# A layer's attention in another order: one block of scores per tile, signals per pair of heads, the adding of x on GpSimd

## The reference

```python
def _L3_xattn_ref(q, k, v, gamma):
    h = N_HEAD                              # 8
    qh = q.reshape(B, h, dq, Lq); kh = k.reshape(B, h, dq, Lk); vh = v.reshape(B, h, dv, Lk)
    qk = jnp.einsum('bhdq,bhdl->bhql', qh, kh) * scale
    sm = jax.nn.softmax(qk, axis=-1)
    ret = jnp.einsum('bhql,bhdl->bhdq', sm, vh)
    return gamma * ret.reshape(B, Dv, Lq)

x = x + jnp.tanh(g_xattn[3]) * _L3_xattn_ref(_layernorm(x, axis=-1), ctx_2048, ctx_2048, L3_xattn_gamma)
```

## Time and profile before

| what | value |
|---|---|
| median of 3 runs | 2855.9 us (2855.89 to 2860.24) |
| the profiled execution, its own time | 2857.04 us |
| its span | 2855.2 us |
| TensorE busy over the span | 2451.8 us (86%) |
| VectorE, ScalarE, GpSimd busy | 2037.1, 1296.4, 1179.1 us |
| mean granted clock of TensorE | 0.931 |
| first score matmul of the stage | at 2593.03 us |
| last statistics of the stage | start at 2818.46 us |

### The profile page before, as it was taken

The page is one execution under the profiler, slowest core; times in us unless marked ns, Lnnn a source line. Parts: engine busy times, 40 slices in busy tenths (PEclk is TensorE's granted clock), DMA queues, the critical chain, the costliest instruction groups (busy, mean ns, idle before and its releaser), DMA issues. The chain is left out here.

```text
span 2855.2 us, 51398 instructions
## 1 busy us (share of the span) xinstructions
PE 2451.8 (86%) x17090; PEld 2057.1 (72%) x17090; DVE 2037.1 (71%) x5105; ACT 1296.4 (45%) x3941; POOL 1179.1 (41%) x2615
## 2 busy tenths in 40 slices
PE   5758999939999999999999869999699997466997
PEld 2346777728888888888888858888588886234775
DVE  7964555558888888888888847777554554895776
ACT  0013333236666666666666623333144443344663
POOL 4401000037777777777777711111143443122112
PEclk9768999969999999999999969999799999676998
DMA  2030000010000000000000030000100000001000
GB/s 73 17 133 24 16 16 8 1 63 3 3 3 5 3 3 3 3 3 3 3 5 1 1 106 23 23 23 12 52 7 9 7 5 1 0 1 53 21 24 31
DMA packets 29155, 56.72 MB, mean 20 GB/s; under 512 B 4846, under 2 KB 22574, under 8 KB 27422
## 3 DMA queue, kind: packets, MB, share of 16 engines
q1 hardware_dynamic: 28894, 53.43, 5.7%
HBM read 51.33 MB, written 2.10 MB: 19 GB/s over the span
## 5 line engine op out<-in xcount | busy, mean ns | idle before, releaser
L434 PE MATMUL bank<-m_xr,m_wgr 128*88 128x512 f32 (+1 forms) x1824 | 442.3, 395 | 17.4 <-POOL m_wgr L494 17.4
L434 PEld LDWEIGHTS bank<-m_xr,m_wgr 128*88 128x88 f32 (+1 forms) x1824 | 307.3, 172 | 116.9 <-issue 19.5
L742 PE MATMUL bank<-l_w,l_xq 128*128 128x128 f32 (+1 forms) x2048 | 358.5, 328 | 9.9 <-DVE l_xq L906 7.1
L742 PEld LDWEIGHTS bank<-l_w,l_xq 128*128 128x128 f32 x2048 | 300.4, 192 | 31.1 <-DVE l_xq L906 7.5
L985 DVE TENSOR_SCALAR xn_T<-xn_T,l_tiny 128x128 f32<-128x128 f32 x768 | 297.2, 453 | 8.4 <-POOL l_tiny L1026 8.4
L494 POOL TENSOR_TENSOR m_wgr<-m_wg,m_wgr 128x512 fp32r<-128x512 f32 (+1 forms) x28 | 40.3, 1440 | 585.5 <-ACT m_wgr L472 585.5
L855 ACT ACTIVATE l_qt<-bank,l_head_b,l_head_w 128x256 f32<-128x256 f32 x256 | 144.6, 565 | 287.5 <-PE bank L787 287.5
L447 PEld LDWEIGHTS bank<-m_wdr,m_hbr 88*128 88x128 f32 (+1 forms) x1824 | 233.1, 192 | 26.9 <-DVE m_hbr L549 18.0
L447 PE MATMUL bank<-m_wdr,m_hbr 88*128 88x256 f32 (+1 forms) x1824 | 239.5, 285 | 10.1 <-DVE m_hbr L549 10.0
L582 DVE SCALAR_TENSOR_TENSOR x_resident<-bank,m_cg,x_resident 128x256 f32<-128x256 f32 x448 | 185.9, 478 | 85.4 <-PE bank L447 79.4
L484 ACT ACTIVATE m_sg<-bank 88x512 f32<-88x512 f32 (+1 forms) x152 | 90.8, 597 | 323.0 <-PE bank L434 323.0
(11 more groups left out here) (272 smaller groups left out, 5715.2 us busy)
## 6 DMA issues: line engine op xcount, KB each, us to landing
l_w<-in_l_w SPq DMA_DIRECT2D x1, 6144.0 KB, 17.3
m_wg<-in_m_gu SPq DMA_DIRECT2D x18, 256.0 KB, 2.6
m_wg<-in_m_gu SPq DMA_DIRECT2D x10, 352.0 KB, 2.9
l2f_w<-in_l_w SPq DMA_DIRECT2D x3, 1024.0 KB, 7.5
m_wd<-in_m_down SPq DMA_DIRECT2D x18, 128.0 KB
x_resident<-in_x SPq DMA_DIRECT2D x4, 512.0 KB, 5.6
l_ctxT<-in_ctxT SPq DMA_DIRECT2D x1, 2048.0 KB, 7.1
l_toep<-in_l_toep SPq DMA_DIRECT2D x16, 128.0 KB, 2.0
```

The source lines that it names most:

```text
L434: r = e.matmul(banks[2 * (q % 2) + half][0:M, :], WGR[:, u % 2, a, k, sub, half, :], XR[:, b, k, cols], start=k == 0 and n == 0, stop=k == ...
L742: e.matmul(bank[:, to:to + width], XQ[:, v, k, :], W[:, k, g, at:at + width], start=k == 0, stop=k == KT - 1)
```

## The change

What it does:

- TensorE issues the scores of all four pairs of a tile in one block of 16 instructions, with `o` as the outer loop. It waits for all exponentials of the tile before.
- Maxima and exponentials are signalled for each pair, four times a tile instead of twice; the first two transpose blocks need the first two pairs only.
- TensorE's order of a step is: two transpose blocks, the next tile's scores, half the values of the tile before, two transpose blocks, the other half. Its pipeline has two tiles in it instead of three.
- VectorE copies block 0 instead of block 3; ScalarE copies 1, 2 and 3, block 3 between the exponentials of the next tile. VectorE's order is four maxima, that copy, the division, then a normalisation or statistics.
- Each tile has its own bank for values, in turn, in place of each batch.
- x is added on GpSimd, behind its cutting of queries and masking of values; the statistics come later.

```diff
-            s_score = signals("scored", 2 * N)
-            s_max = signals("maximum", 2 * N)
-            s_exp = signals("exponent", 2 * N)
+            s_score = signals("scored", N)
+            s_max = signals("maximum", PAIRS * N)
+            s_exp = signals("exponent", PAIRS * N)
...
                 begin(e, ends)
                 for b in range(B):
                     if b >= 2:
-                        e.wait_ge(*s_score(4 * (b - 1)))
+                        e.wait_ge(*s_score(2 * (b - 1)))
                     e.dma_start(CK[:, b % 2, :], A["ctx"][b]).then_inc(s_ck.of(b), 16)
                     if b >= 2:
                         e.wait_ge(*s_cv(b - 1))
                     e.dma_start(CT[:, b % 2, :, :], A["ctxT_b"][b]).then_inc(s_ct.of(b), 16)
...
-            def score(e, n, half):
...
                 if n >= 1:
-                    e.wait_ge(*s_exp(2 * n - 1 + half))
+                    e.wait_ge(*s_exp(PAIRS * n))
                 for o in range(2):
-                    for p in (2 * half, 2 * half + 1):
+                    for p in range(PAIRS):
...
             def turn(e, n, j):
-                e.wait_ge(*s_exp(2 * n + 2))
-                if j >= 2:
-                    e.wait_ge(*s_pte(3 * n + j - 1))
-                elif n >= 1:
-                    e.wait_ge(*(s_pte(3 * n) if j == 0 else s_pte_v(n)))
+                e.wait_ge(*s_exp(PAIRS * n + 2 * a + 2))
+                if j == 0 and n >= 1:
+                    e.wait_ge(*s_pte(3 * (n - 1) + 2))
+                if j == 1 and n >= 1:
+                    e.wait_ge(*s_pte(3 * n))
+                if j == 2:
+                    e.wait_ge(*s_pte_v(n + 1))
+                if j == 3:
+                    e.wait_ge(*s_pte(3 * n + 1))
...
-            def values(e, n):
...
-                e.wait_ge(*s_pte(3 * n + 3))
-                e.wait_ge(*s_pte_v(n + 1))
-                e.wait_ge(*s_cv(b + 1))
-                if qt == 0 and b >= 2:
-                    e.wait_ge(*s_mix(2 * (b - 1)))
-                for o in range(2):
-                    for k in range(KT):
-                        for at, weights in ((0, CV), (D, colm)):
-                            for p in range(PAIRS):
...
+            def values(e, n, o):
+
+                b = n // 2
+                if o == 0:
+                    e.wait_ge(*s_pte(3 * n + 3))
+                    e.wait_ge(*s_pte_v(n + 1))
+                    e.wait_ge(*s_cv(b + 1))
+                    if n >= 2:
+                        e.wait_ge(*s_mix(n - 1))
+                for k in range(KT):
+                    for at, weights in ((0, CV), (P, colm)):
+                        for p in range(PAIRS):
+                            rows = slice(32 * p, 32 * p + 32)
+                            w = CV[:, b % 2, o, k, rows] if weights is CV else colm[:, o, rows]
+                            r = e.matmul(pacc[n % 2][rows, at:at + P], w, PT[:, n % 2, k, 2 * p + o, :],
+                                         start=o == 0 and k == 0 and weights is CV, stop=o == 1 and k == 1 and weights is colm)
+                if o == 1:
+                    r.then_inc(s_pv.sem, 1)
...
             def tensor(e):
                 begin(e, ends)
-                score(e, 0, 0)
-                for s in range(N + 2):
+                score(e, 0)
+                for s in range(N + 1):
                     if s < N:
-                        score(e, s, 1)
-                    if 1 <= s <= N:
-                        turn(e, s - 1, 0)
-                        turn(e, s - 1, 1)
-                    if s >= 2:
-                        values(e, s - 2)
-                    if 1 <= s <= N:
-                        turn(e, s - 1, 2)
+                        turn(e, s, 0)
+                        turn(e, s, 1)
                     if s + 1 < N:
-                        score(e, s + 1, 0)
-                    if 1 <= s <= N:
-                        turn(e, s - 1, 3)
-
-            def exponent(e, n, half):
-                e.wait_ge(*s_max(2 * n + half + 1))
+                        score(e, s + 1)
+                    if s >= 1:
+                        values(e, s - 1, 0)
+                    if s < N:
+                        turn(e, s, 2)
+                        turn(e, s, 3)
+                    if s >= 1:
+                        values(e, s - 1, 1)
+
+            def exponent(e, n, p):
+                e.wait_ge(*s_max(PAIRS * n + p + 1))
                 if n >= 2:
-                for h in range(4 * half, 4 * half + 4):
...
+                for h in (2 * p, 2 * p + 1):
...
                 r.then_inc(s_exp.sem, 1)
...
-                if j < 3:
+                if j == 0:
+                    e.tensor_copy(to, turned[j % 2][:, :]).then_inc(s_pte_v.sem, 1)
+                else:
                     e.copy(to, turned[j % 2][:, :]).then_inc(s_pte.sem, 1)
-                else:
-                    e.tensor_copy(to, turned[j % 2][:, :]).then_inc(s_pte_v.sem, 1)
 
             def scalar(e):
                 begin(e, ends)
                 for s in range(N + 1):
                     if s < N:
                         exponent(e, s, 0)
-                    if s >= 1:
-                        keep_turned(e, s - 1, 0)
-                    if s < N:
                         exponent(e, s, 1)
                     if s >= 1:
-                        keep_turned(e, s - 1, 1)
-                        keep_turned(e, s - 1, 2)
-
-            def maximum(e, n, half):
-                e.wait_ge(*s_score(2 * n + half + 1))
+                        keep_turned(e, s - 1, 3)
+                    if s < N:
+                        exponent(e, s, 2)
+                        exponent(e, s, 3)
+                        keep_turned(e, s, 1)
+                        keep_turned(e, s, 2)
+
+            def maximum(e, n, p):
+                e.wait_ge(*s_score(n + 1))
                 if n >= 2:
-                    e.wait_ge(*s_exp(2 * (n - 2) + half + 1))
-                for p in (2 * half, 2 * half + 1):
-                    r = e.tensor_reduce(negmax[:, n % 2, 2 * p:2 * p + 2], scores[p][:, :].rearrange("p (o k) -> p o k", o=2),
-                                        AXX, ALU.max, negate=True)
-                r.then_inc(s_max.sem, 1)
-
-            def finish(e, n):
-                b, qt = n // 2, n % 2
-                cols = slice(qt * P, (qt + 1) * P)
+                    e.wait_ge(*s_exp(PAIRS * (n - 2) + p + 1))
+                e.tensor_reduce(negmax[:, n % 2, 2 * p:2 * p + 2], scores[p][:, :].rearrange("p (o k) -> p o k", o=2),
+                                AXX, ALU.max, negate=True).then_inc(s_max.sem, 1)
+
+            def divide(e, n):
                 e.wait_ge(*s_pv(n + 1))
-                e.reciprocal(rinv[:, n % 2, :], pacc[b % 2][:, D + qt * P:D + (qt + 1) * P]).then_inc(s_inv.sem, 1)
+                e.reciprocal(rinv[:, n % 2, :], pacc[n % 2][:, P:2 * P]).then_inc(s_inv.sem, 1)
                 e.wait_ge(*s_inv(n + 1))
                 if n >= 2:
                     e.wait_ge(*s_xadd(n - 1))
-                e.scalar_tensor_tensor(mixed[:, n % 2, :], pacc[b % 2][:, cols], gam[:, 0:1], rinv[:, n % 2, :],
+                e.scalar_tensor_tensor(mixed[:, n % 2, :], pacc[n % 2][:, 0:P], gam[:, 0:1], rinv[:, n % 2, :],
                                        ALU.mult, ALU.mult).then_inc(s_mix.sem, 1)
-                e.wait_ge(*s_mix(n + 1))
-                e.tensor_tensor(X[:, b, cols], X[:, b, cols], mixed[:, n % 2, :], ALU.add).then_inc(s_xadd.sem, 1)
-                if qt == 1:
-                    e.wait_ge(*s_xadd(n + 1))
-                    e.bn_stats(stats[:, b, :], X[:, b, :]).then_inc(bn.sem, 1)
...
-                for s in range(N + 2):
-                    if s == 0:
-                        maximum(e, 0, 0)
+                for s in range(N + 4):
                     if s < N:
-                        maximum(e, s, 1)
-                    if s >= 2:
-                        finish(e, s - 2)
+                        for p in range(PAIRS):
+                            maximum(e, s, p)
+                        keep_turned(e, s, 0)
+                    if 2 <= s < N + 2:
+                        divide(e, s - 2)
                     if s % 2 == 1 and s // 2 + 2 < B:
                         normalise(e, s // 2 + 2)
-                    if s + 1 < N:
-                        maximum(e, s + 1, 0)
-                    if 1 <= s <= N:
-                        keep_turned(e, s - 1, 3)
+                    if s >= 4 and s % 2 == 0:
+                        b = s // 2 - 2
+                        e.wait_ge(*s_xadd(2 * b + 2))
+                        e.bn_stats(stats[:, b, :], X[:, b, :]).then_inc(bn.sem, 1)
...
             def gpsimd(e):
                 begin(e, ends)
-                for b in range(B):
...
+                separate(e, 0)
+                for s in range(N + 2):
+                    if s % 2 == 0 and s // 2 + 1 < B:
+                        separate(e, s // 2 + 1)
+                    if s >= 2:
```

(47 more changed lines are left out.)

1 line of the change is left out of this document (removed).

## The result

The changed kernel takes **2864.76 us**, the kernel before in the same runs 2857.82 (14 runs each): a ratio of 1.0025, 95% interval 1.0016 to 1.0033, or 6.9 us slower. The forecast was 3.8 slower, 2859.7, with a range of 2851 to 2873 that holds the result. Of its three cases the result falls, with 6.9, just beyond the line of 5.7 us: into "slower", which had 0.42, and not into "within", which had 0.48. Of the 5.1 us between 2859.7 and 2864.76 the change makes up 3.1; the other 1.9 are the kernel before, whose median is 2857.82 in these 14 runs and was 2855.9 in the three that the forecast started from.

The account below looks back on a forecast made before the run. TensorE bound the stage before; afterwards a TensorE–ScalarE ring of 6.85 us a step would. Steps +7.1, start -0.5, end -2.8 give +3.8 us on the 2855.9 median: 2859.7, range 2851 to 2873.

Parts of the forecast that it names:

- the line of 5.7 us: About 0.2% of the kernel's time, what a measurement of this kernel can tell from no change; passed with steps over 6.92.
- slower: Whole kernel: slower than before by more than 5.7 us; chance 0.42.
- within: Whole kernel: within 5.7 us of the time before; chance 0.48.
- The ring: Fourth layer's attention: TensorE and ScalarE wait for each other through ScalarE's second copy; 6.85 us a step instead of 6.595.
- TensorE's own work: Per step after the change: scores 1.10, values 2.00, transposes 2.12, together 5.22 us; not the bound.
- The rivals with poor overlap: Score blocks: four groups run in full succession, 2889 us, chance 0.03, or overlap in part, 2867 us, chance 0.06.
- the rival: TensorE's idle 1.6 us a step lowers the clock; about 2902 us, or 2865 to 2875 for a few steps; chance 0.10.
- Start and end: Stage's first and last tiles, partly at 1.2 GHz: start -0.5 us, end -2.8 us, as the pipeline is a step shorter.
- VectorE fits: VectorE's maxima, copy, division and normalisation or statistics fit inside the step, covered by 1.4 us of slack.
- GpSimd's add: Adding x on GpSimd, between 0.29 and 0.73 us, is hidden in each step; only the last tile's lies on the path.
- The rival on the faster side: TensorE stays the bound with steps of 5.2 to 5.6 us: 2815 up to 2826 us; chance 0.08.

## Why the prediction was right, and where it was off

**The ring.** It was named link by link, in the right order, and every link is in the timeline. 6.85 was forecast, 6.93 measured. The 0.08 come mostly from one choice: for the last four exponentials I took the row at 2711.46, 1.57 long, while those that follow a copy directly are the row at 2707.13, 1.61; measured 1.62. The rest is a hundredth here and there, in the scores, the values, the transposes and the first copy. 28 x 0.08 = 2.3 us.

**TensorE's own work and the four row groups.** The block of 16 scores takes 1.15 us from its first start to its last end, where a half block of 8 took 1.13. To what follows it is 1.11, forecast 1.10. The rivals with poor overlap, 2867 and 2889, are out. The Trainium skill (TensorE: Matmul & The Clock Gate, Part 3, Measured speedup vs the span model) gives a speedup of 3.07 for four row tiles. That isn't what these rows show: 8 instructions on two groups took 1.07 to what follows, so 16 on one group would take 4 x 1.07 = 4.28 if two groups overlap fully, and 4.28 / 3.07 = 1.39, as an estimate from the page's figure, is 0.28 longer than the 1.11 measured.

**The clock.** This is the step that failed, in part: the sum has nothing for a fall of the clock, and two cost 3.1 us. The forecast had 1.00 in the middle of the stage and gave the rival 0.10, with "a few such steps give 2865 to 2875". It came in its mild form, in two of the 28 steps from tile 3 to tile 31, with 1.57 each. My argument against it was that TensorE had been far idler where the clock had fallen before, 1.19 busy of 3.40 us, than 5.2 of 6.85. That is an average over a step, and within a step the idle time is bunched: just ahead of the fall at 2685.40 it was busy 1.85 of 3.40 us. The windows of the earlier trace rows had shown the clock rise behind nothing but transposes, and the added transposes bear that out: with them the falls are gone. The Trainium skill (TensorE: Matmul & The Clock Gate, Part 4), by which transposes don't count as activity, isn't borne out.

**Start and end.** 24.6 us to tile 3's scores were forecast, 23.56 measured: the clock rose for the second time at 2610.31, and the first values were done in part at 2.4 GHz. The forecast had taken 1.2 GHz for them. From tile 31's scores to the end 13.3 were forecast and 13.3 measured.

The sum over the stage, in the execution profiled: forecast +3.8; the ring's error +2.3, two falls +3.1, the start -1.0; together +8.2, as measured. Over the whole execution it is 7.7, as the stage began 1.0 earlier and the rest ran 0.5 longer; in the medians it is 6.9, since the profiled execution of the kernel before, 2857.04, lies 0.8 under its median. That the error of the sum stayed at 4.4 is in part luck: the start came out 1.0 better than forecast while the ring and the clock came out 5.4 worse.

**The other engines.** That VectorE fits was right: it had 0.27 us to spare, and the undone add shows how tight that is. Costing GpSimd's add at nothing was right; it took 0.45 to 0.55, between the bounds 0.29 and 0.73.

**The rival on the faster side**, TensorE as the bound, was left because of ScalarE's queue, and the experiments say that was the right reason: moving one copy brings steps of 6.08, moving one half of the values 5.92, both together 6.07. The version at 5.42 has three edits (TensorE's order, ScalarE's copies behind all eight exponentials, block 3 on VectorE); which of the latter two it needs isn't shown.

What stays open: what exactly decides about a fall. The two lie behind the least busy windows of the stage (1.85 and 1.86 of 3.4 us), and they come at the same tiles with x on VectorE, so they are hardly chance; but behind equally idle windows, as at 2675.17, there was none. Both kernels were traced once, so how often the falls come in other executions isn't known.

## What to carry to other kernels

When an order is written out by hand, look for rings: an instruction that starts the next round, and all that stands ahead of it in its queue, followed back until one comes to its own engine again. The sum of the links along the longest ring bounds the step, whatever the busy times say. An instruction in that ring costs its whole length, until another ring is longer, and one outside costs nothing as long as it fits. Gains from cutting two rings don't add; the longer one left over is the next step's length. And what a part is worth can depend on the rest: moving the adding to GpSimd, together with a later place for the statistics, is worth 11 us with the old order, and undoing the move of the adding costs nothing with the new one.

## What the hardware did that was not expected

- Between tile 3 and tile 31 the clock fell to 1.2 GHz twice, each time for 3.4 us, though TensorE never idled for more than 0.85 us at a time there (1.05 between its weight loads) and was busy 127.20 of the 164 us in the middle. With four transposes without use in each step, 0.44 us of work, no fall is left.
- At the start of the stage the clock rose to 2.4 GHz 11.5 us after the first scores, fell again at 14.9 behind 3.4 us in which TensorE was busy 1.41, and rose at 18.3; before the change it rose once, after 21.9, and stayed up to the end of the stage.
- Four row groups of 32 run side by side: at 2.4 GHz 16 instructions of 256 columns took 1.15 us, where 8 in two groups took 1.13.
